# Attention scores from fp32 row tiles, exponentials over four banks, and the sums of the softmax from a column of ones

## The reference, cut to what matters

```
Q = t rot Wq^T;  K = t ent Wk^T;  V = t Wv^T
scores = exp(-(|q|^2 + |k|^2 - 2 q.k))
x = x + softmax(scores) V          # exp of an exp, divided by its sum over the keys
```

## Time and profile before

| | |
|---|---|
| median of 3 runs | 221.15 us (219.72 to 221.16) |
| profiled execution | 221.34 us |
| its span, first to last instruction | 219.4 us |
| busy PE / DVE / ACT / POOL | 89% / 73% / 77% / 14% |
| moved by DMA | 21.95 MB |

### The profile page before, as it was taken

How to read it: one execution, slowest core, us unless ns; L and a number is a source line. 1 busy time by engine, 2 the same in 40 slices (tenths; PEclk the granted TensorE clock), 3 DMA queues, 4 the chain that set the end, 5 groups by cost and what they waited for, 6 DMA issues and landing times. The chain is left out here.

```text
span 219.4 us, 3503 instructions
## 1 busy us (share of the span) xinstructions
PE 194.5 (89%) x1178; PEld 99.0 (45%) x1178; DVE 160.8 (73%) x298; ACT 169.8 (77%) x323; POOL 29.8 (14%) x44
## 2 busy tenths in 40 slices
PE   6875999999999997889999999999999999389950
PEld 6842646546555444323334343434343333168840
DVE  0449549999999954995958396877778695676990
ACT  4055499699779799997998989999998984377740
POOL 7000000190060061080203010101001000000000
PEclk9999999999999999979999999999999999999996
DMA  6940110176429350393443617080620000000016
GB/s 185 358 148 29 39 40 0 9 247 173 123 112 264 95 224 19 132 261 81 111 122 76 152 39 192 0 207 24 168 60 3 0 0 0 0 3 3 0 64 237
DMA packets 20213, 21.95 MB, mean 100 GB/s; under 512 B 2046, under 2 KB 17086, under 8 KB 20068
## 3 DMA queue, kind: packets, MB, share of 16 engines
q1 hardware_dynamic: 20196, 21.73, 34.2%
HBM read 14.74 MB, written 6.96 MB: 99 GB/s over the span
## 5 line engine op out<-in xcount | busy, mean ns | idle before, releaser
L507 ACT ACTIVATE arena<-ps 128x800 f32<-128x800 f32 (+1 forms) x56 | 44.6, 798 | 5.8 <-PE ps L1064 5.3
L514 ACT ACTIVATE arena<-arena 128x800 f32<-128x800 f32 (+1 forms) x56 | 46.4, 831 | 0.0
L1064 PE MATMUL ps<-qa,ka 128*128 128x400 bf16 (+1 forms) x128 | 35.4, 340 | 2.1 <-ACT arena L507 2.1
L1064 PE MATMUL ps<-qb,kb 96*128 96x400 bf16 (+1 forms) x128 | 35.4, 339 | 0.0
L741 DVE TENSOR_TENSOR psum<-arena 128x400 f32<-128x400 f32 x32 | 19.6, 612 | 14.2 <-ACT arena L514 14.2
L741 DVE TENSOR_TENSOR psum<-psum,arena 128x400 f32<-128x400 f32 x32 | 19.5, 608 | 6.1 <-ACT arena L514 4.7
L1064 PEld LDWEIGHTS ps<-qa,ka 128*128 128x128 bf16 (+1 forms) x128 | 10.4, 97 | 26.1 <-ACT arena L507 12.4
L1097 PE MATMUL ps<-arena,vb 128*32 128x400 f32 x192 | 21.6, 525 | 0.3 <-issue 0.3
L750 DVE RECIPROCAL arena<-ps 128x400 f32<-128x400 f32 x7 | 18.6, 2650 | 0.0
L660 DVE COPY arena<-arena 32x400 f32<-32x400 f32 x48 | 17.2, 358 | 0.9
L1182 PE MATMUL ps<-yb,cst 128*128 128x120 f32 (+1 forms) x102 | 15.1, 283 | 1.4 <-ACT yb L597 0.6
(11 more groups left out here) (151 smaller groups left out, 359.6 us busy)
## 6 DMA issues: line engine op xcount, KB each, us to landing
ka<-dk SPq DMA_DIRECT2D x32, 100.0 KB
qa<-dq SPq DMA_DIRECT2D x32, 100.0 KB
dk<-arena SPq DMA_DIRECT2D x8, 300.0 KB, 2.2
dq<-arena SPq DMA_DIRECT2D x8, 300.0 KB, 2.6
arena<-x_tok SPq DMA_DIRECT2D x4, 400.0 KB
t<-x SPq DMA_DIRECT2D x1, 1600.0 KB, 11.6
kb<-dk SPq DMA_DIRECT2D x16, 100.0 KB
qb<-dq SPq DMA_DIRECT2D x16, 100.0 KB
```

The costliest lines, as they stand in the source:

```text
L507: nc.scalar.activation(prob[par][:, lo:hi, :], ps[:, o:o + hi - lo, 0:N], ACT.Exp, scale=2.0).then_inc(e1_done, 1)
L514: nc.scalar.activation(p, p, ACT.Exp).then_inc(p_ready, 1)
L1064: last = mm_(ps[row:row + keys, bank, 0:N], kk[par][0:rows, b, o:o + keys], qq[par][0:rows, b, :], start=first, stop=not first, skip_group ...
```

## The change

- Scores: K and Q stay in SBUF as fp32 (`kf`, `qf`). A unit is now one key tile of all four images: four fp32 matmuls with the 32 channels of an image as rows, each on its own 32 rows of the array and into its own bank (0 to 3), and then four bf16 matmuls with six rows that add the squares (`ek`, `eq`). A group has three units and a tail (bank 4). The next unit waits for the inner exponential of the unit before.
- ACT: one instruction spans four banks (128x1600); the tails have their own. The Square of the second norm moves to DVE (`squares2`) but for the last groups.
- The splitting into parts, its stores and its loads are gone; the squares are still split by POOL and go through DRAM into `ek`, `eq`.
- Values: the product takes the normalised tokens themselves (`value_products` with the identity), of which channel 31 is replaced by ones. Tokens sum to zero over the channels, so channel 31 follows from the others and W2 = rest Wv^T. Row 31 of a product is then the sum of the softmax: `unscaled` copies the product to SBUF, `mix_values` multiplies by W2, and the sums reach all rows through DRAM (`spread_sums` on SP: one store, four broadcasts) or, for the last two groups, by a matmul (`spread_sums` on PE). The adds, `sums` and `tail_sums` are gone.
- For the last three groups, W2's products, the projections and the norms have banks of their own (`LAST_W2`, `LAST_WX`, `LAST_NORM`) and further tiles for squares and roots.
- In the last pair, DVE copies K, Q and the values while ACT squares.

```diff
-        NORM_BANKS = (6, 7)
-        LAST_BANKS = {G - 2: (0, 1), G - 1: (2, 3)}
+        TAIL_BANK, PV_BANK, SUM_BANK, NORM_BANK = 4, 5, 6, 7
+        LAST_W2, LAST_WX, LAST_NORM = {G - 2: 0, G - 1: 1}, {G - 3: 3, G - 2: 0, G - 1: 5}, {G - 2: 2, G - 1: 4}
...
# SP
+            def spread_sums(g):
+                sp.wait_ge(us_ready, g + 1)
+                sp.dma_start(scaled[g], us[g % 2][:, :]).then_inc(sums_out, 16)
+                sp.wait_ge(sums_out, 16 * (g + 1))
+                if g > 0:
+                    sp.wait_ge(rden_ready, g)
+                for b in range(NB):
+                    sp.dma_start(sums[C * b:C * b + C, :],
+                                 scaled[g, C * b + C - 1:C * b + C, :].partition_broadcast(C)).then_inc(sums_in, 16)
+            for g in range(G - 2):
+                spread_sums(g)
...
# ACT
+            def inner(g, q):
+                act.wait_ge(s_done, FULL * g + q + 1)
+                nc.scalar.activation(prob[g % 2][:, NB * q:NB * q + NB, :], ps[:, 0:NB, 0:N], ACT.Exp,
                                      scale=2.0).then_inc(e1_done, 1)
...
+            def weights(g):
+                if g > 1:
                     act.wait_ge(pv_done, g - 1)
+                inner(g, 0)
+                inner_tail(g - 1)
+                outer(g - 1, 2)
+                outer_tail(g - 1)
+                inner(g, 1)
+                if g > 2:
+                    norm2(g - 3, 1)
+                    norm2(g - 3, 2)
+                outer(g, 0)
+                inner(g, 2)
+                outer(g, 1)
+            squares(PAIRS - 1)
+            inner(0, 0)
+            inverse_roots(PAIRS - 1)
+            inner(0, 1)
+            outer(0, 0)
+            kq_squares(PAIRS - 1)
+            inner(0, 2)
+            outer(0, 1)
+            e_copies(PAIRS - 1)
             for g in range(1, G):
+                weights(g)
+            inner_tail(G - 1)
+            outer(G - 1, 2)
+            outer_tail(G - 1)
+            last_reciprocals(G - 2)
+            norm2(G - 3, 0)
+            last_reciprocals(G - 1)
             for step in range(1, 3):
                 norm2(G - 3, step)
+            norm2(G - 2, 0)
+            norm2(G - 1, 0)
+            for g in range(G - 2, G):
+                for step in range(1, 3):
+                    norm2(g, step)
...
# DVE
+            for g in range(1, G):
+                if g > 1:
+                    reciprocals(g - 2)
+                    quotient(g - 2)
+                    residual(g - 2)
+                unscaled(g - 1)
+                if g > 2:
+                    project2(g - 3)
+                    stats(g - 3)
+                if 1 < g < G - 1:
+                    squares2(g - 2)
+            quotient(G - 2)
+            residual(G - 2)
+            unscaled(G - 1)
             project2(G - 3)
             stats(G - 3)
+            quotient(G - 1)
+            residual(G - 1)
+            for g in range(G - 2, G):
+                project2(g)
+                stats(g)
...
# PE
+            def scores(g, q):
+                if q == 0:
+                    pe.wait_ge(k1_ready, g + 1)
+                    pe.wait_ge(q1_ready, g + 1)
+                    pe.wait_ge(e_in[g // 2], 16 * E_LOADS)
+                if FULL * g + q:
+                    pe.wait_ge(e1_done, FULL * g + q)
+                for b in range(NB):
+                    mm_(ps[:, b, 0:N], kf[C * b:C * b + C, g, P * q:P * q + P], qf[C * b:C * b + C, g, :],
+                        start=True, stop=False)
+                for b in range(NB):
+                    r = slice(C * b, C * b + 2 * EP)
+                    last = mm_(ps[:, b, 0:N], ek[r, g, P * q:P * q + P], eq[r, g, :], start=False, stop=True)
                 last.then_inc(s_done, 1)
...
+            center(PAIRS - 1)
+            scores(0, 0)
+            variance(PAIRS - 1)
+            scores(0, 1)
+            project_kq(PAIRS - 1)
+            scores(0, 2)
+            project_v(PAIRS - 1)
+            scores(1, 0)
...
+            for g in range(1, G):
+                scores(g, 1)
+                if g > 2:
+                    variance2(g - 3)
+                products(g - 1, 1)
+                if g > 1:
+                    mix_values(g - 2)
+                scores(g, 2)
+                if g > 2:
+                    project2(g - 3)
+                products(g - 1, 2)
+                tail_products(g - 1)
+                if g < G - 1:
+                    scores(g + 1, 0)
+                    tail_scores(g)
+                    if g > 1:
                         center2(g - 2)
+                    products(g, 0)
+            tail_scores(G - 1)
+            spread_sums(G - 2)
+            products(G - 1, 0)
+            products(G - 1, 1)
+            mix_values(G - 2)
+            products(G - 1, 2)
+            tail_products(G - 1)
+            center2(G - 3)
+            spread_sums(G - 1)
+            mix_values(G - 1)
+            project2(G - 3)
+            variance2(G - 3)
+            center2(G - 2)
+            center2(G - 1)
+            variance2(G - 2)
+            variance2(G - 1)
+            project2(G - 2)
+            project2(G - 1)
```

More of the change, by code:

```diff
@@ L141, in build @@
         xl = [piece(N) for _ in range(2)]
[L142 to L145, removed]
+        cut[0] = at_1 + PROB
+        rden = piece(N)
         es = piece(N)
@@ L559, in _ @@
-            for step, first, end in ((squares, 0, 2), (inverse_roots, 2, 3), (kq_firsts, 3, 5),
-                                     (v_and_squares, 5, UNITS)):
-                step(PAIRS - 1)
-                for u in range(first, end):
-                    inner(0, 0, u)
-                    if u:
-                        outer(0, 0, u - 1)
-            for g in range(1, G):
-                weights(g, g % 2)
-            outer(G - 1, 1, UNITS - 1)
+                inner(g, 0)
+                inner_tail(g - 1)
@@ L1067, in scores, with tail_scores @@
                 last.then_inc(s_done, 1)
[L1069 to L1073 removed]
+            def tail_scores(g):
+                if g > 0:
+                    pe.wait_ge(et_done, g)
                 for b in range(NB):
[L1075 to L1077 removed]
@@ L1121, in _ @@
-            PRODUCTS_AT = (1, 2, 4, 5)
-            def attend(g, par):
-                since = g if isinstance(g, int) else G
-                for u in range(UNITS):
-                    scores(g, par, u)
-                    if since > 0 and u in PRODUCTS_AT:
-                        products(g - 1, 1 - par, PRODUCTS_AT.index(u), first=since == 1)
-                    if since > 0 and u == 3:
-                        sums(g - 1, 1 - par, first=since == 1)
-                        tail_sums(g - 1, 1 - par)
-                    if since > 1 and u == 4:
-                        center2(g - 2)
-                    if since > 1 and u == 5:
-                        project2(g - 2)
-                    if since > 1 and u == 6:
-                        variance2(g - 2)
@@ L1141, in _ @@
-            pe.wait_ge(operands_in[0], LOADED)
-            for step, first, end in ((center, 0, 2), (variance, 2, 3), (project_kq, 3, 5), (project_v, 5, UNITS)):
-                step(PAIRS - 1)
-                for u in range(first, end):
-                    scores(0, 0, u)
-            pe.wait_ge(v_ready, G + CREDIT)
-            pe.wait_ge(es_ready, G + CREDIT)
-            for g in range(1, G):
-                pe.wait_ge(operands_in[g % 2], LOADED * (g // 2 + 1))
-                attend(g, g % 2)
@@ L1151, in _ @@
-            for k in range(2):
-                products(G - 1, 1, k, False)
-            center2(G - 2, LAST_BANKS[G - 2])
-            sums(G - 1, 1, False)
-            tail_sums(G - 1, 1)
-            for k in range(2, FULL + 1):
-                products(G - 1, 1, k, False)
-            variance2(G - 2, LAST_BANKS[G - 2])
-            project2(G - 2, LAST_BANKS[G - 2])
-            center2(G - 1, LAST_BANKS[G - 1])
-            variance2(G - 1, LAST_BANKS[G - 1])
-            project2(G - 1, LAST_BANKS[G - 1])
+                mm_(ps[:, bank, 0:N], c_("mean"), squares_of.get(g, sq2), start=True, stop=True).then_inc(var2_done, 1)
```

520 lines of the change are left out of this document (220 added, 300 removed).

## The result

The changed kernel takes 215.07 us (median of four runs, 213.64 to 217.62) against 221.09 for the kernel before (219.72 to 221.16): ratio 0.971, 95% interval 0.965 to 0.977. Predicted were 213.6 us and a range of 207 to 224. The profiled run took 213.92 us with a span of 212.1; the forecast span was 211.7.

The account below looks back on a forecast made before the run. PE was taken to set the attention's pace, with ACT close behind. Span 219.4 - 0.7 (convolution) - 3.8 (transition) - 7.8 (loop) + 4.6 (end) = 211.7, plus 1.9 around it: 213.6 us, range 207 to 224.

Parts of the forecast that it names:

- TensorE sets the loop, 11.0 us a group: Attention loop: PE's matmuls and twelve switches sum to 11.0 us per group, against 12.07 before.
- Row tiles overlap like column tiles: Score units: four matmuls on row tiles overlap as the column quad does, 0.95 us per unit.
- the estimate by the page's figure: Score units: the skill page's 3.07x for four row tiles adds 0.14 us per unit, 216 in all.
- ScalarE at 10.2, under TensorE; 9.3 in groups 1 and 2: Attention loop: ACT needs 10.2 us per group, below PE's 11.0; in groups 1 and 2 ACT sets 9.3.
- Sums through DRAM, hidden: Loop: 10.1 us from the copy to center2, with 13.2 available, so hidden with 3 us to spare.
- rival 4: Loop: broadcasts landing 5 us later stall center2 on PE by 2 us in six groups, 225.6, slower; chance 0.07.
- A reciprocal that waits on a DMA: Sign in the trace after: a reciprocal waiting on DMA would make the prediction wrong.
- Convolution -0.7: Convolution: DVE's relief is mostly spare time; 0.2 us per pair, 0.7 in all, bounds 0 and 2.
- Transition 15.1: From center(3) to group 1's first exponential: 15.1 us instead of 18.9, 3.8 less.
- End 17.0: Last exponential's start to last stats' end: 17.0 us instead of 12.4, grows by 4.6, bounds +2 and +6.
- The sum: Whole span: 219.4 - 0.7 - 3.8 - 7.8 + 4.6 = 211.7 us.
- loop 76.1 (75.4 predicted): Group 1's first exponential to the last exponential: 75.4 us instead of 83.2, 7.8 less.

Follow-up runs that it names:

- doubled centering: Changed kernel with the second centering matmul of groups 0 to 4 issued twice: 217.84 us, ratio 0.976 to the kernel before.
- halved exponentials: Changed kernel with each exponential over 1600 elements issued as two over 800: 215.84 us.
- grouped order: Changed kernel with TensorE's fp32 128x128 matmuls placed together in each group, nothing added or left out: 214.46 us, ratio 0.969 to the kernel before.
- control: The changed kernel itself, unchanged, run once more beside other experiments: 214.68 us, ratio 0.969 to the kernel before.
- the swap: Changed kernel with quotient and residual of group 7 ahead of project2 and stats of group 5: 210.14 us, ratio 0.949 to the kernel before.
- the run with twelve: Changed kernel with twelve unread VectorE subtractions per convolution pair, eight of them behind add_x and ahead of y_copy: 228.11 us.
- the run with the work in its old places: Changed kernel with unread VectorE work per convolution pair where the kernel before had its splitting, part of it behind y_copy: 216.06 us.

## Why the prediction was right

- **TensorE sets the loop, 11.0 us a group:** 10.91 from group 3 on. Terms close to the predicted: a unit with its switch 1.07 (1.05 measured), a lone matmul 0.77 and a switch 0.12 (0.87), a quad of products 0.67 and 0.12 (0.81). The doubled centering shows that TensorE's time goes through, the halved exponentials that ScalarE's doesn't, the grouped order that switches with their loads are part of the sum.
- **Row tiles overlap like column tiles:** shown by taking them away. The fp32 quad takes 0.77 against 2.82 in single file, 3.7 times faster. The Trainium skill, TensorE: Matmul & The Clock Gate ("Packing small matmuls — row/col tiling"), gives 3.07 for four row tiles. This trace is better than that. The total alone would not have decided it: the estimate by the page's figure was 216, and the medians are 215.07 and 214.68.
- **ScalarE at 10.2, under TensorE; 9.3 in groups 1 and 2:** 9.33, and 0.47 us idle in each later group, where about 1 was expected. So its own pace there is 10.91 - 0.47 = 10.44; Ln and Exp of the norm take 1.07 and not 0.9. The grouped order, at 10.52, is within 0.1 us of it, so little more can be gained on TensorE there. The four-bank exponentials have pitches of 1.38 to 1.40 and 1.42 to 1.43 (1.39 and 1.43 predicted). The Trainium skill, TensorEngine Tiling (Array Packing) ("PSUM Bottleneck"), says that the emptying of PSUM may become the bottleneck once tiling has sped up TensorE. Here ScalarE, which empties it, is the pace in groups 1 and 2 alone.
- **Sums through DRAM, hidden:** in all groups but one. In a usual group the step's numbers hold: group 4's residual ends 9.7 us behind its copy (142.57 to 152.30; 10.1 predicted), 3.1 before center2 (155.41). In group 1 they don't:

```profile
121.70 0.85 DVE L741 TENSOR_TENSOR ul<-ps,prep 128x400 f32<-128x400 f32 x1
...
122.70 0.91 PE L1087 MATMUL ps<-t,cst 128*128 128x400 f32 x2 [1.16 <-DVE ul L741]
```

  center2 of group 1 waits 1.16 us (0.72 in the control) for VectorE's project2 of group 0, which frees its bank and stands behind the late reciprocal of group 1. That is the long period, 1.2 and 0.75 us of the span. The step counted on one landing time and on periods of 11.0 for all groups. But group 0's chain from copy to residual takes 11.1 us (99.12 to 110.19) in a period of 9.33, so group 1's copy, behind it on VectorE, starts 1.7 late; and then its sums take 0.8 (control) to 1.4 us longer to land than those of groups 0 and 2. It is rival 4's mechanism once instead of six times. A reciprocal that waits on a DMA was named as a sign against the forecast; it does wait, 1.7 to 2.2 us in the later groups, but TensorE doesn't wait for it there.
- **Convolution -0.7, with VectorE's relief mostly spare:** a pair lost 0.25 (0.2 taken), the wait of TensorE for L689 that is gone; the rest of VectorE's work there was spare time. center(3) comes 0.63 earlier.
- **Transition 15.1:** 76.25 (76.88 in the earlier trace rows) to 91.09, 14.8. The sum counted it from TensorE's instructions; no run took its 4 us apart.
- **End 17.0 with quotient 7 behind stats 5, bounded by 2 us of clock:** 16.6 without the clock's fall and 18.1 with it; the swap shows the mechanism. The fall in the earlier trace rows on which the bound rests stands behind a wait of 1.7 us (to 94.09), not of 3.
- **The sum:** 211.7 against spans of 212.1 and 213.9. That the first is within 0.4 is in part luck, since its misses cancel: loop 76.1 (75.4 predicted), recurrence 28.3 (28.0), transition 14.8 (15.1), end 16.6 (17.0).

What the prediction left on the table is in its own text: it named the quotient behind the stats. Ready at 172.96, it starts at 176.55, and one exchange of lines makes the end 3.1 to 4.6 us shorter.

## What to carry to other kernels

When one engine is busy without a gap, price a change by the starts of its instructions, switches of tile shape and unhidden weight loads included; relief for the other engines counts only where the first waits for them. On an in-order engine look at the end of a pipeline for ready work behind work that waits: a wait of some 3 us of TensorE there can cost twice, once as itself and, as in the control, once by the granted clock. And work that costs nothing in one place may cost all of itself a few lines further up.

## What was not expected of the hardware

The granted clock fell to 1.2 GHz without an idle stretch. With score matmuls on 32 rows in single file it fell between 80 and 85 (0.75), behind the first such unit, with TensorE busy 5.00 of 5 us there and in the 5 before (1.00); from 110 to 120 it was 0.50 at 10.00 of 10. With two row tiles side by side it is 1.00 from 90 to 170, with four from 72 to 167.

VectorE and POOL held each other up on tiles in SBUF. Of the eight subtractions in the run with twelve, the four that begin ahead of POOL's steps took 0.56 each, the four that begin behind the start of one 1.22 to 1.31, each ending 0.43 behind the end of that step. POOL's steps themselves took 1.02 to 1.15, against 0.85 and 0.94 in the changed kernel. The first of these pairs:

```profile
44.22 1.02 POOL L340 TENSOR_TENSOR arena<-arena,cst 128x400 bf16<-128x400 f32 x1 [2.40 <-ACT arena L444]
...
44.45 1.22 DVE L691 TENSOR_TENSOR spare<-cst 128x400 f32<-128x400 f32 x1
```

In the run with the work in its old places it went the other way: a step of POOL that takes 0.94 took 2.25 and ended 0.8 behind VectorE's last subtraction (45.51), whose two took 0.56 each.

```profile
44.06 2.25 POOL L343 TENSOR_TENSOR arena<-arena 128x400 f32<-128x400 f32 x1
...
44.47 1.04 DVE L688 TENSOR_TENSOR spare_b<-cst 128x400 bf16<-128x400 f32 x2
```

These rows look like one engine waiting for the other to be through, not like both running slower. What decides which of the two waits no run took apart.

The late sums of group 1 come with a packet of the instruction queue. In the changed kernel, the transfers' issue and the reciprocal that waits for them, then the DMA queues from 114 to 115:

```profile
112.66 2.90 SPq L297 DMA_DIRECT2D sums<-scaled  x4
...
117.37 2.65 DVE L714 RECIPROCAL arena<-sums 128x400 f32<-128x400 f32 x1 [4.66 <-DMA sums<-scaled]
```

```profile
q8 instruction: 1, 0.02, 7.1%
```

4.71 us from issue to reciprocal, where groups 0 and 2 take 3.26 and 3.29. In eleven profiles, all but the two with fewer row tiles, it was 3.98 to 4.79, each time with such a packet in between. With two row tiles the groups are longer, the packet fell between 121.1 and 121.2, next to the reciprocal's start, and the sums took 3.30:

```profile
117.89 1.71 SPq L297 DMA_DIRECT2D sums<-scaled  x4
...
121.19 2.65 DVE L714 RECIPROCAL arena<-sums 128x400 f32<-128x400 f32 x1 [1.47 <-DMA sums<-scaled]
```

That the packet delays them fits all of these, but no run moved it alone.
